# Row copies, load order and an early top-2 in a three-stage transformer kernel

## The chip, the cores and the metric

One core of one Trainium2 chip runs the whole program. The metric is the device time of one launch in microseconds (us). All tensors are float32 in DRAM.

## What is computed

Four sequences of 512 tokens of width 512 (2,048 rows) go through a mixture of experts, an attention layer, and the same mixture again, each with a residual sum:

```python
x = L0_attn_hidden_states                                     # (4, 512, 512)
x = x + 0.5 * ffn(layernorm(x), W_gate, b_gate, W_e, b_e)     # 8 experts, top 2
x = x + attn(layernorm(x), Wqkv, q_ln_w, q_ln_b, k_ln_w, k_ln_b, Wout)
x = x + 0.5 * ffn(layernorm(x), W_gate, b_gate, W_e, b_e)

# ffn: the two experts with the largest logits, their outputs averaged
logits = x @ W_gate + b_gate
_, top_idx = top_k(logits, 2)
y_all = relu(einsum('bsd,edh->bseh', x, W_e) + b_e)
y = take_along_axis(y_all, top_idx[..., None], axis=2).mean(axis=2)
# attn: 32 heads of 16, q and k clipped and layer-normed, ALiBi, causal softmax
```

## The kernel before

The program has three parts, each a block in which the five engines run their own instruction lists and meet at semaphores.

**First routing and first experts (0 to 238 us).** `route_block` (L1007, here with `proj` False) normalises the 16 tiles of 128 rows in 8 pairs and computes gate logits, the top 2, and lists that sort the (row, expert) pairs into 39 tiles of 128 slots. `expert_block` (L1588) gathers the normalised rows of a slot tile, multiplies them with one expert's weights and adds the result to the rows in `acc` with an indirect DMA. In the routing, SP's list (`sync`, L1188) does for pair u: load x for pair u+2 (L1128), store the normalised pair u-1 (L1145), load two pieces of expert weights (L1156), and store the raw pair u to `acc` (`store_x`, L1139), since the expert outputs are added there. A pair's buffer (4 of them, `XR`, which are the buffer of the expert biases) is loaded anew only when the store of its last content has landed (L1127). DVE's list (`vector`, L1453) does the statistics, 11 short steps of an inverse root, and two TENSOR_SCALARs (L1484) for each pair. ACT rounds each weight piece to its high part (L1404), and POOL subtracts it to get the low part (L1263), 16 pieces in all. PE transposes the pair (L1296), multiplies with the gate (`gate`, L1302) and turns the logits back (`turn_logits`, L1311), two pairs behind. When all 16 tiles have their logits, DVE picks the top 2 for all of them at once: 16 instructions (L1493 to L1507), and then PE ranks them (L1362 to L1365). The weights of the attention (`load_wq`, L1203) are loaded and turned in the gaps.

**Projection and attention (238 to 727 us).** `qkv_block` (L231) walks the 16 tiles. DVE's `unit(t)` (L478) begins with the statistics of the x tile t+2 (L485), which waits for that tile's load; then come the clip, the norms of q and k, and the normalised x of tile t+2. SP's `step(t)` (L310) does: store the four q and k pieces of tile t-2 (L308), load x of tile t+3 (L295), store v of tile t (L299). From tile 8 to 11 each step is followed by 14 DMAs that load a group's stacks (`load_fixed` with 6, L207, and `load` with 8, L218). `attention_block` (L571) walks NG = 32 groups of 4 heads. PE's iteration n (L806) has the scores with keys on partitions for group n (L758), the scores for the row maxima of group n+2 (L733), and the values of group n-1 (L771). The row maxima of group n+1 go: PE turns them (L742), ACT copies them to `m_rows` (L849), SP sends them into the q stack of that group by four small DMAs (`max_rows`, L631), and PE's first L758 of iteration n+1 waits for those (L749). SP's list for iteration n is: fixed rows of group n+4 (while n < 4), stack of group n+4, v of group n+2, `max_rows(n+1)`, and in some iterations a store (L639) and loads for the second routing (`sync_early`, L1163, from n = 16 to 24).

**Second routing and second experts (727 to 982 us).** The same functions with `proj` True: the routing also multiplies with the output weights and adds x (L1447), and stores the sum (L1141).

## Time and profile before

| | us |
|---|---|
| runs of the kernel before | 970.96, 975.37, 982.41 |
| median | 975.37 |
| profiled execution | 983.81 |
| its span from the first to the last record | 982.0 |
| PE busy in it | 841.5 |
| DVE, ACT, POOL busy in it | 632.4, 449.1, 446.1 |

The span begins with the first instruction that the profiler records and ends with the last one; 1.8 us of the execution lie around it. Busy time says little here, since the stages have different limits. Each stage is read by its own rows: which engine never waits, and who waits for whom at the step that is repeated.

### The profile page before, as it was taken

Reading aid. Unit: us, or ns where it says so; the run is one execution under the profiler, and the core shown is the slowest. Engines: PE = TensorE matmul, PEld = TensorE weight load, DVE = VectorE, ACT = ScalarE, POOL = GpSimd, SP = SyncE. Lnnn points to the kernel's source line nnn. Section 1 sums busy time; section 2 is a strip of 40 time slices with the busy share of each in tenths; the row PEclk is TensorE's granted clock in tenths of the full one; section 3 lists DMA queues with packets and bytes.
Section 4 is the critical chain, followed back from the end, with each engine's and each line's share of the span. In section 5 each row is a group of like instructions: output and inputs, shape, how many; then the busy total and the mean of one; then the engine's idle time right before and its main releaser. Section 6 shows DMA issues by size and latency. Waiting matters only on the chain. (4 is left out here: it accounts for less than half of the span.)

```text
span 982.0 us, 18936 instructions
## 1 busy us (share of the span) xinstructions
PE 841.5 (86%) x5922; PEld 592.5 (60%) x5923; DVE 632.4 (64%) x1289; ACT 449.1 (46%) x834; POOL 446.1 (45%) x565
## 2 busy tenths in 40 slices
PE   3666999993989998878899999889989983899995
PEld 1344888872677777655455555445557752788874
DVE  7966344333978877776688887678728768344432
ACT  3541333332244443347577777577754430233331
POOL 7732677764022222224243344235446431577764
PEclk9785999996899999978899999899999995899998
DMA  9985677863264689665667679898239940578874
GB/s 341 387 300 175 124 148 145 149 118 53 54 197 150 196 199 230 195 196 127 146 139 154 143 154 189 165 192 178 54 107 321 323 161 32 123 144 152 149 133 62
DMA packets 113255, 164.54 MB, mean 168 GB/s; under 512 B 16929, under 2 KB 74401, under 8 KB 112897
## 3 DMA queue, kind: packets, MB, share of 16 engines
q1 hardware_dynamic: 95328, 126.40, 46.6%
q0 software_dynamic: 17856, 37.25, 20.4%
q8 instruction: 39, 0.64, 0.3%
q14 instruction: 32, 0.25, 0.1%
HBM read 100.05 MB, written 68.68 MB: 172 GB/s over the span
## 5 line engine op out<-in xcount | busy, mean ns | idle before, releaser
L901 DVE TENSOR_REDUCE att_part<-att_s_ps 128x2 f32<-128x1024 f32 (+2 forms) x160 | 195.2, 1225 | 46.4 <-PE att_s_ps L733 42.4
L858 ACT ACTIVATE att_prob<-att_st_ps 128x512 f32<-128x512 f32 x320 | 174.2, 598 | 75.3 <-PE att_st_ps L758 71.2
L687 POOL TENSOR_SCALAR_AFFINE_SELECT att_prob<-att_prob 128x256 f32<-128x256 f32 (+1 forms) x224 | 93.7, 442 | 108.0 <-ACT att_prob L858 107.9
L153 PE MATMUL exp_z_ps<-ex_w_hi,exp_xT_hi 128*128 x312 | 132.4, 424 | 1.7 <-issue 1.3
L155 PE MATMUL exp_z_ps<-ex_w_hi,exp_xT_lo 128*128 x312 | 124.8, 400 | 0.0
L154 PE MATMUL exp_z_ps<-ex_w_lo,exp_xT_hi 128*128 x312 | 124.7, 400 | 0.0
L1684 ACT ACTIVATE exp_y<-exp_y 128x512 f32<-128x512 f32 x72 | 45.5, 632 | 170.5 <-DVE exp_y L1703 142.0
L1691 DVE TENSOR_TENSOR exp_xT_lo<-exp_t_ps,exp_xT_hi 128x512 fp32r<-128x512 f32 x78 | 53.9, 692 | 99.8 <-ACT exp_xT_hi L1675 81.2
L1263 POOL TENSOR_TENSOR ex_w_lo<-ex_w_lo,ex_w_hi 128x1024 fp32r<-128x1024 f32 x32 | 77.0, 2418 | 78.0 <-ACT ex_w_hi L1404 41.6
L771 PE MATMUL att_pv_ps<-att_prob,att_v_sb 128*32 128x256 f32 (+2 forms) x1280 | 103.2, 397 | 1.6 <-ACT wt_w_turned L863 1.6
L153 PE MATMUL qkv_o_ps<-qkv_w_hi,qkv_xT_hi 128*128 128x512 f32 x192 | 82.6, 430 | 2.4 <-DVE qkv_xT_lo L464 1.6
L154 PE MATMUL qkv_o_ps<-qkv_w_lo,qkv_xT_hi 128*128 128x512 f32 x192 | 78.6, 409 | 0.0
L155 PE MATMUL qkv_o_ps<-qkv_w_hi,qkv_xT_lo 128*128 128x512 f32 x192 | 78.0, 406 | 0.0
L1640 POOL DMA_INDIRECT out<-exp_y,ex_row_of x39 | 61.9, 1588 | 34.5 <-DMA out<-exp_y,ex_row_of 12.9
L363 POOL TENSOR_TENSOR st_partq<-qkv_wholeq,st_partq 128x512 fp32r<-128x512 f32 x16 | 20.7, 1293 | 124.9 <-ACT st_partq L435 124.9
L153 PEld LDWEIGHTS exp_z_ps<-ex_w_hi,exp_xT_hi 128*128 128x128 f32 x312 | 61.0, 195 | 15.7 <-issue 4.7
L155 PEld LDWEIGHTS exp_z_ps<-ex_w_hi,exp_xT_lo 128*128 128x128 f32 x312 | 60.0, 192 | 14.4
L1640 POOL DMA_INDIRECT acc<-exp_y,ex_row_of x33 | 52.4, 1589 | 33.4 <-issue 16.9
L154 PEld LDWEIGHTS exp_z_ps<-ex_w_lo,exp_xT_hi 128*128 128x128 f32 x312 | 60.5, 194 | 10.8
L712 PE MATMUL att_s_ps<-st_masks 64*128 64x256 bf16 (+1 forms) x640 | 58.9, 264 | 4.2 <-DVE att_part L901 4.2
L1675 ACT ACTIVATE exp_xT_hi<-exp_t_ps 128x512 fp32r<-128x512 f32 x78 | 45.4, 582 | 36.3 <-PE exp_t_ps L1652 36.3
L712 PEld LDWEIGHTS att_s_ps<-st_masks 64*128 64x128 bf16 x640 | 18.9, 97 | 61.5 <-issue 53.6
(206 smaller groups left out, 1618.2 us busy)
## 6 DMA issues: line engine op xcount, KB each, us to landing
ex_w_lo<-in_L_ffn_W_e SPq DMA_DIRECT2D x32, 512.0 KB, 6.7
v_vals<-st_vals SPq DMA_DIRECT2D x16, 512.0 KB, 2.9
q_parts<-st_partq SPq DMA_DIRECT2D x32, 256.0 KB, 3.6
k_parts<-st_partk SPq DMA_DIRECT2D x32, 256.0 KB, 4.0
att_v_sb<-v_vals SPq DMA_DIRECT2D x32, 256.0 KB, 3.8
ex_bias<-in_L_attn_hidden_states SPq DMA_DIRECT2D x8, 512.0 KB, 7.4
acc<-ex_bias SPq DMA_DIRECT2D x8, 512.0 KB, 8.3
xn<-ex_rows SPq DMA_DIRECT2D x8, 512.0 KB, 5.5
```

Of the source, the lines that this page charges most:

```text
L153: nc.tensor.matmul(out, x_hi[:, s], w_hi(c), start=(c == 0), stop=False)
L154: nc.tensor.matmul(out, x_hi[:, s], w_lo(c), start=False, stop=False)
L155: last = nc.tensor.matmul(out, x_lo[:, s], w_hi(c), start=False, stop=(c == C - 1))
L687: last = nc.gpsimd.affine_select(out=block, in_=block, compare_op=ALU.is_ge, fill=0.0, base=0, pattern=[[0, block.shape[1]], [1, P]], chan ...
L712: nc.tensor.matmul(blocks_of(banks[half], where), mine[:, 0, :], rhs, start=(c == 0), stop=False, skip_group_check=True)
L771: last = nc.tensor.matmul(pv_ps[VW * h:VW * (h + 1), j * P + c0:j * P + c1], v_sb[n % RING][:, j, VW * h:VW * (h + 1)], prob[n % 2][:, col ...
L858: nc.scalar.activation(prob[n % 2][:, col:col + 512], st_ps[(e + half) % 3][:, :], ACT.Exp).then_inc(exp_done, 1)
L901: nc.vector.tensor_reduce(out, src, X_AXIS, ALU.max, negate=True).then_inc(red_done, 1)
L1263: nc.gpsimd.tensor_tensor(ex.w_lo[:, 2 * n:2 * n + 2, :], ex.w_lo[:, 2 * n:2 * n + 2, :].bitcast(F32), ex.w_hi[:, 2 * n:2 * n + 2, :].bitc ...
L1640: nc.gpsimd.indirect_dma_start(out=acc[:, :], out_offset=bass.IndirectOffsetOnAxis(ap=ex.row_of[:, s:s + 1], axis=0), in_=y[s % RING], in_ ...
L1684: nc.scalar.activation(y[r], y[r], ACT.Relu, scale=0.25).then_inc(y_done, 1)
L1691: nc.vector.tensor_tensor(xT_lo[r % 2][:, :], t_ps[r % 2][:, :], xT_hi[r % 2][:, :].bitcast(F32), ALU.subtract).then_inc(lo_done, 1)
```

## The change

- **A.** First routing: `store_x` is gone from the loop. x rows reach `acc` by four DRAM-to-DRAM copies of 1 MB each (`copy_rows`), two behind the last store of normalised rows and two after the fourth piece of attention weights. The x loads no longer wait for stores, and neither does the load of the expert biases.
- **B.** Both routings: the top 2 are picked in two goes, for tiles 0 to 13 as soon as the seventh pair's logits are turned (after a copy of these logits to SBUF), and for tiles 14 and 15 after the last pair. PE turns the seventh pair's logits before it transposes the last pair. The buffer of the turned logits is now shared with the later one-hot columns and no longer with the picks.
- **C.** `qkv_block`: SP loads x of tile t+3 before it stores q and k of tile t-2.
- **D.** `attention_block`: `max_rows(n+1)` heads SP's iteration, before the stack and v loads, and takes two DMAs and not four; for this the maxima's high and low parts lie in another order in `m_parts`.

```diff
@@ qkv_block, sync @@
             def step(t, par):
+                if not (isinstance(t, int) and t + 3 >= TILES):
+                    load_x(t + 3, 1 - par)
                 if after(t, 2):
                     store_qk(t - 2, par)
-                if not (isinstance(t, int) and t + 3 >= TILES):
-                    load_x(t + 3, 1 - par)
                 store_v(t, par)
@@ attention_block, sync @@
                 for half, base in halves():
-                    for part_of in range(2):
-                        row = base + SCORE_ROWS + part_of
-                        src = m_rows[n % 2][4 * part_of + 2 * half:4 * part_of + 2 * half + 2, :]
-                        sp.dma_start(q_st[n % SLOTS][row:row + 1, :, :].bitcast(F32), src.bitcast(F32)).then_inc(m_loaded[n % 2], 16)
+                    row = base + SCORE_ROWS
+                    src = m_rows[n % 2][HG * half:HG * (half + 1), :]
+                    sp.dma_start(q_st[n % SLOTS][row:row + MAX_ROWS, :, :].bitcast(F32), src.bitcast(F32)).then_inc(m_loaded[n % 2], 16)
...
             for n in range(NG):
+                if n + 1 < NG:
+                    max_rows(n + 1)
                 if n + AHEAD < SLOTS:
                     st.load_fixed(sp, n + AHEAD)
                 if n + AHEAD < NG:
                     load(n + AHEAD)
                 if n + 2 < NG:
                     load_v(n + 2)
-                if n + 1 < NG:
-                    max_rows(n + 1)
@@ attention_block, gpsimd @@
-                flat = part[n % 2][:, :, :, :].rearrange("p a b s -> p (a b) s")
-                nc.gpsimd.tensor_copy(m_parts[n % 2][:, 0, :, :], flat).then_inc(m_hi_done, 1)
+                whole, parts = part[n % 2][:, :, :, :], m_parts[n % 2]
+                nc.gpsimd.tensor_copy(parts[:, :, 0, :, :], whole).then_inc(m_hi_done, 1)
                 pool.wait_ge(m_hi_done, n + 1)
-                nc.gpsimd.tensor_tensor(m_parts[n % 2][:, 1, :, :], flat, m_parts[n % 2][:, 0, :, :].bitcast(F32),
+                nc.gpsimd.tensor_tensor(parts[:, :, 1, :, :], whole, parts[:, :, 0, :, :].bitcast(F32),
                                         ALU.subtract).then_inc(m_lo_done, 1)
@@ route_block @@
-    lgT = work[0:E, 0:2 * P]
...
-    at_col = tables.sb("at_col", [P, COL_RING, P], BF16)
+    turning = tables.sb("turning", [P, 2 * P])
+    lgT = turning[0:E, :]
+    at_col = turning[:, :].bitcast(BF16).rearrange("p (r n) -> p r n", r=COL_RING)
...
     def load_x(u):
         if u >= XR:
             sp.wait_ge(xn_done, 2 * (u - XR) + 2)
-            sp.wait_ge(x_stored[u % XR], 16 * (u // XR))
+            if proj:
+                sp.wait_ge(x_stored[u % XR], 16 * (u // XR))
@@ route_block, sync @@
-            store_x(u)
+            if proj:
+                store_x(u)
...
+        def copy_rows(i):
+            part = slice(i * (TOKENS // XR), (i + 1) * (TOKENS // XR))
+            sp.dma_start(acc[part, :], x_in[part, :]).then_inc(x_stored[i], 16)
...
         store_xn(PAIRS - 1)
-        for i in range(XR):
-            sp.wait_ge(x_stored[i], 16 * (PAIRS // XR))
+        if not proj:
+            copy_rows(0)
+            copy_rows(1)
+        if proj:
+            for i in range(XR):
+                sp.wait_ge(x_stored[i], 16 * (PAIRS // XR))
         sp.wait_ge(xn_done, TILES)
         sp.dma_start(ex.bias[:, :], b_e.rearrange("(a e) h -> a (e h)", a=1).to_broadcast([P, E * D])).then_inc(ex.bias_loaded, 16)
         if w_qkv is not None:
-            for n in range(2, WQ_PAIRS):
-                load_wq(n)
+            load_wq(2)
+            load_wq(3)
+            copy_rows(2)
+            copy_rows(3)
+            load_wq(4)
+            load_wq(5)
@@ route_block, tensor @@
+            if u == PAIRS:
+                turn_logits(u - 2)
             if 1 <= u <= PAIRS:
                 transpose(2 * u - 2)
                 transpose(2 * u - 1)
-            if u >= 2:
+            if u >= 2 and u != PAIRS:
+                if u == PAIRS + 1:
+                    pe.wait_ge(lg_kept, 1)
                 turn_logits(u - 2)
@@ route_block, vector @@
+        kept = over[:, :, :].rearrange("p e t -> p (e t)").rearrange("p (t e) -> p t e", e=E)
+        def picks(t0, t1, first):
+            n, three = slice(t0, t1), [P, t1 - t0, E]
...
+            for k, source in enumerate((first, rest)):
+                chain(nc.vector.tensor_reduce(best[:, n, 0], source[:, n, :], X_AXIS, ALU.max))
+                chain(nc.vector.tensor_tensor(eq[:, n, :], source[:, n, :], best[:, n, :].to_broadcast(three), ALU.is_equal))
...
+            nc.vector.tensor_tensor(pair[:, n, 1, :], picked[:, n, :], pair[:, n, 0, :], ALU.subtract).then_inc(picked_done, 1)
+        dve.wait_ge(gate_done, PAIRS - 1)
+        nc.vector.tensor_copy(kept[:, 0:TILES - 2, :], logits[:, 0:TILES - 2, :]).then_inc(lg_kept, 1)
+        dve.wait_ge(lg_kept, 1)
+        picks(0, TILES - 2, kept)
         dve.wait_ge(gate_done, PAIRS)
...
+        picks(TILES - 2, TILES, logits)
```

`picks` has the 16 instructions of L1493 to L1507, each on tiles t0 to t1 only. The waits for `picked_done` (PE before the ranks, POOL before its last weight piece) now ask for 2 and not 1, and PE's and ACT's waits for `m_loaded` for 32 in each group and not 64.

## Rows read from the trace of the kernel before

**Rows 1.** Window 25 to 50 us: busy us of each engine, granted clock, DMA share, GB/s

```profile
25.00:50.00 25.00, 17.26 (x69) 8.52 (x68) 23.07 (x64) 13.25 (x20) 19.03 (x9) 0.73 0.99 380
```

**Rows 2.** Timeline of the routing loop: start us, us, engine, line, operation [idle before]

```profile
27.85 4.83 POOL L1263 TENSOR_TENSOR ex_w_lo<-ex_w_lo,ex_w_hi 128x1024 fp32r<-128x1024 f32 x2 [0.30 <-ACT ex_w_hi L1404]
...
29.32 3.65 DVE L1484 TENSOR_SCALAR ex_rows<-ex_bias,route_mv,route_rstd 128x512 f32<-128x512 f32 x2
...
57.21 1.00 DVE L1484 TENSOR_SCALAR ex_rows<-ex_bias,route_mv,route_rstd 128x512 f32<-128x512 f32 x2
```

**Rows 3.** 0 to 62 us: a group (busy, mean ns), a wait (total, times, longest)

```profile
L1484 DVE TENSOR_SCALAR ex_rows<-ex_bias,route_mv,route_rstd 128x512 f32<-128x512 f32 x16 | 21.8, 1403 | 0.3
...
ACT ex_w_hi L1404 <- DMA ex_w_lo<-in_L_ffn_W_e: 29.4, 9, 7.7
```

**Rows 4.** Timeline at the end of the first routing

```profile
59.95 0.29 PE L1315 MATMUL route_g_ps<-ex_ident,route_work 8*128 8x8 f32 x2
...
63.59 0.29 DVE L1493 TENSOR_REDUCE route_best<-route_g_ps 128x16 f32<-128x128 f32 x1 [5.38 <-PE route_g_ps L1315]
...
68.45 0.29 DVE L1507 TENSOR_TENSOR route_pair<-route_eq,route_pair 128x128 bf16<-128x128 f32 x1
...
71.34 0.17 DVE L1511 TENSOR_TENSOR route_counts<-route_totals 128x8 f32<-128x8 f32 x1
...
86.42 1.05 POOL L965 DMA_INDIRECT ex_rows<-xn,ex_token_of  x1 [15.19 <-DVE ex_token_of L1551]
```

**Rows 5.** Timeline at the end of the second routing: the first pick

```profile
810.60 0.29 DVE L1493 TENSOR_REDUCE route_best<-route_g_ps 128x16 f32<-128x128 f32 x1 [5.91 <-PE route_g_ps L1315]
```

**Rows 6.** DMA issues: a 2 MB copy within DRAM, us from issue to landing

```profile
bias_rows<-in_bias_rows SPq DMA_DIRECT2D x1, 8.8
```

**Rows 7.** Projection: SP's queue and DVE in time, tiles 7 to 9; last the total wait

```profile
339.30 0.34 SPq L299 DMA_DIRECT2D v_vals<-st_vals  x1
...
349.61 0.34 SPq L299 DMA_DIRECT2D v_vals<-st_vals  x1
...
356.07 0.98 SPq L308 DMA_DIRECT2D q_parts<-st_partq  x2
...
358.49 2.03 SPq L295 DMA_DIRECT2D qkv_x<-acc  x1
...
364.15 0.69 DVE L485 BATCH_NORM_STATS2 qkv_stats<-qkv_x 128x6 f32<-128x512 f32 x1 [4.18 <-DMA qkv_x<-acc]
...
DVE qkv_stats L485 <- DMA qkv_x<-acc: 14.0, 5, 4.2
```

**Rows 8.** Attention in time: ACT's maxima, SP's sending, PE's waits; last PE's total

```profile
457.38 0.57 ACT L849 ACTIVATE att_m_rows<-att_s_ps 8x512 fp32r<-8x512 f32 x1
...
474.91 0.57 ACT L849 ACTIVATE att_m_rows<-att_s_ps 8x512 fp32r<-8x512 f32 x1
...
478.69 2.38 SPq L637 DMA_DIRECT2D att_q_st<-att_m_rows  x4
...
482.22 0.79 PE L758 MATMUL att_st_ps<-att_q_st,att_k_st 64*128 64x512 f32 x2 [2.24 <-DMA att_q_st<-att_m_rows]
...
495.75 0.57 ACT L849 ACTIVATE att_m_rows<-att_s_ps 8x512 fp32r<-8x512 f32 x1
...
520.54 0.57 ACT L849 ACTIVATE att_m_rows<-att_s_ps 8x512 fp32r<-8x512 f32 x1
...
629.57 0.80 PE L758 MATMUL att_st_ps<-att_q_st,att_k_st 64*128 64x512 f32 x2 [3.28 <-DMA att_q_st<-att_m_rows]
...
711.00 0.57 ACT L849 ACTIVATE att_m_rows<-att_s_ps 8x512 fp32r<-8x512 f32 x1
...
  PE att_st_ps L758: 10.7, 9
```

**Rows 9.** Attention, windows without and with the routing's early weights (columns as Rows 1)

```profile
504.00:512.30 8.30, 7.87 (x103) 4.33 (x101) 6.87 (x8) 6.30 (x14) 3.33 (x10) 1.00 0.71 141
...
604.00:613.00 9.00, 8.01 (x108) 4.36 (x100) 6.98 (x9) 6.38 (x14) 3.40 (x9) 1.00 1.06 192
```

More of the change, by code:

```diff
@@ L581, in attention_block @@
         part = [m.sb(f"part{i}", [P, 2, 2, SEGS]) for i in range(2)]
-        m_parts = [m.sb(f"m_parts{i}", [P, 2, 4, SEGS], F32R) for i in range(2)]
+        m_parts = [m.sb(f"m_parts{i}", [P, 2, 2, 2, SEGS], F32R) for i in range(2)]
         m_rows = [m.sb(f"m_rows{i}", [2 * HG, SEQ], F32R) for i in range(2)]
@@ L607, in attention_block @@
         STACK_LOADS, FIXED_LOADS = 8, 6
+        MAX_LOADS = 16 * 2
         def ring_unit(k):
@@ L1489, in vector @@
         dve.wait_ge(const_done, 12)
-        dve.wait_ge(gate_done, PAIRS)
-        three = [P, TILES, E]
-        for k, source in enumerate((logits, rest)):
-            chain(nc.vector.tensor_reduce(best[:, :, 0], source[:, :, :], X_AXIS, ALU.max))
-            chain(nc.vector.tensor_tensor(eq[:, :, :], source[:, :, :], best[:, :, :].to_broadcast(three), ALU.is_equal))
-            chain(nc.vector.scalar_tensor_tensor(val[:, :, :], eq[:, :, :], -100.0, n_expert[:, :, :], ALU.mult, ALU.add))
-            chain(nc.vector.tensor_reduce(low[:, :, 0], val[:, :, :], X_AXIS, ALU.min))
-            chain(nc.vector.tensor_tensor(pick[k][:, :, :], val[:, :, :], low[:, :, :].to_broadcast(three), ALU.is_equal))
-            if k == 0:
-                chain(nc.vector.scalar_tensor_tensor(rest[:, :, :], pick[0][:, :, :], NEG, logits[:, :, :], ALU.mult, ALU.add))
@@ L1503, in vector @@
-        chain(nc.vector.tensor_tensor(picked[:, :, :], pick[0][:, :, :], pick[1][:, :, :], ALU.add))
-        chain(nc.vector.scalar_tensor_tensor(val[:, :, :], picked[:, :, :], -100.0, n_expert[:, :, :], ALU.mult, ALU.add))
-        chain(nc.vector.tensor_reduce(low[:, :, 0], val[:, :, :], X_AXIS, ALU.min))
-        chain(nc.vector.tensor_tensor(pair[:, :, 0, :], val[:, :, :], low[:, :, :].to_broadcast(three), ALU.is_equal))
-        nc.vector.tensor_tensor(pair[:, :, 1, :], picked[:, :, :], pair[:, :, 0, :], ALU.subtract).then_inc(picked_done, 1)
+        kept = over[:, :, :].rearrange("p e t -> p (e t)").rearrange("p (t e) -> p t e", e=E)
@@ new lines, in picks @@
+        def picks(t0, t1, first):
[3 more added lines that the diff above has]
+                chain(nc.vector.tensor_tensor(eq[:, n, :], source[:, n, :], best[:, n, :].to_broadcast(three), ALU.is_equal))
+                chain(nc.vector.scalar_tensor_tensor(val[:, n, :], eq[:, n, :], -100.0, n_expert[:, n, :], ALU.mult, ALU.add))
+                chain(nc.vector.tensor_reduce(low[:, n, 0], val[:, n, :], X_AXIS, ALU.min))
+                chain(nc.vector.tensor_tensor(pick[k][:, n, :], val[:, n, :], low[:, n, :].to_broadcast(three), ALU.is_equal))
+                if k == 0:
+                    chain(nc.vector.scalar_tensor_tensor(rest[:, n, :], pick[0][:, n, :], NEG, first[:, n, :], ALU.mult, ALU.add))
+            chain(nc.vector.tensor_tensor(picked[:, n, :], pick[0][:, n, :], pick[1][:, n, :], ALU.add))
+            chain(nc.vector.scalar_tensor_tensor(val[:, n, :], picked[:, n, :], -100.0, n_expert[:, n, :], ALU.mult, ALU.add))
+            chain(nc.vector.tensor_reduce(low[:, n, 0], val[:, n, :], X_AXIS, ALU.min))
+            chain(nc.vector.tensor_tensor(pair[:, n, 0, :], val[:, n, :], low[:, n, :].to_broadcast(three), ALU.is_equal))
+            nc.vector.tensor_tensor(pair[:, n, 1, :], picked[:, n, :], pair[:, n, 0, :], ALU.subtract).then_inc(picked_done, 1)
```

15 lines of the change are left out of this document (8 added, 7 removed).

## The prediction

> **What bounds the kernel now.** I read the windows first, then for each stage the waits, the timeline, and SP's queue.
>
> In the first routing DMA and DVE are both nearly full: 0.99 of the DMA engines' time and 23.07 of 25 us of DVE [rows 1]. The reader should see in the timeline which of them sets the end. DVE never waits in the loop after its first load; its normalising pair takes 1.00 us when POOL is idle, and 3.65 us when it starts inside two of POOL's weight pieces [rows 2]. All 16 TENSOR_SCALARs took 21.8 us [rows 3], at 0.50 us each it would be 8.0: 13.8 us of the loop is DVE standing behind POOL. DMA shows only as ACT's wait for weights, 29.4 us in nine [rows 3], off the path by itself. So the loop's end is set by DVE and POOL, not by the bytes.
>
> Behind the loop one chain runs to the first gather: logits, 16 picks from 63.59 to 68.74, ranks, lists, gather at 86.42 [rows 4]. The second routing has it too, from 810.60 on [rows 5].
>
> In the projection SP's v stores show the beat: 10.31 us for an undisturbed tile [rows 7]. Five times DVE waits for x, 14.0 us in all, 4.18 us at 364.15; that load was issued at 358.49, behind 14 stack loads and the q and k stores that began at 356.07 [rows 7].
>
> In the attention the undisturbed beat, from one of ACT's copies of maxima to the next, is 8.26 us (three from 495.75 to 520.54), with PE busy 7.87 of 8.30 us [rows 8, 9]. From 457.38 to 711.00 there are 29 beats in 253.6 us, 14.0 more than 29 x 8.26; the first four of them lose 5.3 (38.4 against 33.1) [rows 8]. PE waits nine times for maxima, 10.7 us, the longest 3.28 at 629.57 [rows 8]; this is most of the 14.0. There are two causes. At 478.69 SP sends maxima that ACT had ready at 475.48 [rows 8], since SP was still issuing 15 loads: late by 3.2 us. And in iterations with early weights the DMA share is 1.06 against 0.71 [rows 9], so the four small DMAs land behind a backlog.
>
> **A, the copies.** Removed: eight 512 KB stores. Added: four 1 MB copies. The 2 MB copy of the bias rows took 8.8 us from issue to landing [rows 6], so 4 MB are at most 17.6 us. They lie between 58 and 86 us beside 2 MB of biases and 2 MB of attention weights; these 8 MB at the loop's 380 GB/s [rows 1] are 22 us, which ends at about 80, before the gather at 86.42 [rows 4]. Cost nothing; if this cover is gone, the gather shares the engines with a tail of a few us, and I take 0 to +3. In the loop 4 of about 20 MB go, so weights land sooner and ACT and POOL start sooner; POOL still has its 15 pieces of 2.4 us. By the bytes the loop could shrink by 4.2 MB / 380 GB/s = 11 us; by the lock it shrinks only as far as fewer pieces fall on a pair. ACT's list puts the odd piece of each step behind the copies of the newest pair, so it still runs when the next pair is normalised, while the even piece can move ahead of it. So most of the 13.8 us stays: I take a fifth, rounded down to -2.5, with ends +2 (pieces can also fall worse, as the 3.65 shows) and -11.
>
> A rule that speaks against a gain by bytes stands in the Trainium skill, "SBUF — State Buffer", section "Who interferes with whom": VectorE and GpSimd share a pair of ports as an exclusive lock, and a TENSOR_SCALAR in its two-port mode blocks or is blocked for a whole instruction. By that rule the trace agrees (3.65 against 1.00 us), and A alone would give about nothing in the loop; by the bytes it would give 11.
>
> **B, the picks.** 16 instructions at 128x128 take 0.29 us, started every 0.32; at 16 columns they cost what L1511 does, 0.17 and 0.03 between, so 0.20 [rows 4]. The last go saves 16 x 0.12 = 1.9 us if the first go (a copy and 16 instructions at 112 columns, 5.2 us) fits before the last logits. Second routing: DVE is free at 804.69, since it idles 5.91 us before 810.60 [rows 5]; the first go ends at 809.9. It fits: -1.9. First routing: the seventh pair's logits were turned at 59.95 behind the transposes [rows 4], now at about 59.6; the first go ends at 65.1 and the second at 68.4, against 68.74. The transposes start 0.9 us later, but the last logits are still there in time. -0.3, up to -1.9 if the seventh gate product runs at 2.4 GHz: I take -0.7.
>
> **C, the x load.** SP would issue it at 356.07, not at 358.49, and 1 MB of stores is no longer ahead. Before, DVE had it 5.7 us after its issue [rows 7]; 1 MB at 380 GB/s is 2.8 us, so it takes about 3 and arrives near 359.0, where DVE wanted it at 359.97. What waits behind it on SP, the q and k stores, is wanted by nobody for two tiles; their engines have 10 us. So the 14.0 us should mostly go. But tiles 8 to 11 keep their 14 stack loads each, whose bytes are still ahead of x, and as the beats get shorter they press harder: I take 9 of the 14, ends -3 (only one of the five waits goes) and -12.
>
> **D, the maxima.** Two DMAs of the same kind save 2 x 0.6 = 1.2 us of SP's time per group (2.38 us for four [rows 8]). In iterations 0 to 3 SP issues 6 fixed, 8 stack and 1 v loads; the same 14 took 6.1 us in the projection (349.95 to 356.07 [rows 7]), 15 are 6.6, and with 2.4 that is 9.0 us against a beat of 8.26. With 7.8 us, and the maxima first, SP is never late: this gives back the 5.3 us. PE wants the maxima 4.5 us after ACT's copy (480.0 against 475.5 [rows 8]); in the iterations with early weights they have 3.3 us for landing then, not 2.1. The DMA share of 1.06 there [rows 9] says that a backlog stays, so of the other 8.7 us I take half, -4.3. POOL's two small instructions and PE's turn keep their sizes. D: -9.6, ends -3 and -14.
>
> The price of D: the stack of group n+4 and v are queued behind the wait for maxima n+1, some 6 us later than now. The stack is issued by 1.2 + 3.5 = 4.7 us after ACT's copy (7.3 with the fixed rows), and PE's L733 of group n+4 wants it a beat after the maxima, at 12.8. Cover: 8.1 us (5.5 in the first four) against 5.7 for a load behind a full queue [rows 7]. I cost it at nothing; without the cover each us late is a us in every group.
>
> **Sum.** -2.5 - 0.7 - 1.9 - 9 - 9.6 = -23.7 us on the profiled 983.8, that is 960.1, or 2.4%. The profiled execution is the slowest of the four times seen, and presumably has more of these waits; on the median of 975.4 I take nine tenths, 21 us: **954 us**.
>
> **Rivals.**
> 1. The backlog keeps the waits. For it: DMA share 1.06 [rows 9] and the full projection tiles; against it: the x load leaps over a megabyte. Only one x wait (14.0 / 5 = 2.8), SP's lateness (5.3) and B (2.6) are saved, about 11 us: 964.5 us.
> 2. Routing is DMA-bound after all and A gives its 11 us and not 2.5: 8.5 us more, 945.5 us. For it: 0.99; against it: DVE never idles.
> 3. Slower: the stacks come late (D). In iterations 0 to 27, each L733 of group n+2 would wait for its stack. It costs from a landing above 8.1 us after the last issue, and decides from 9.0, where 24 iterations eat the 21 us. At 9.6 it costs 36, and the kernel ends at 975.4 - 21 + 36 = 990 us. Against it: the 5.7 of [rows 7]; for it: the share of 1.06 [rows 9].
>
> The "Measured" table of the Trainium skill's "DMA: Bandwidth & Descriptors" (section "Bandwidth") gives 6.15 us for 1 MB, which puts the four copies at 24.6 us as an estimate, one after another; no run here shows it.
>
> **How the numbers follow.** My forecast 0.72, rival 1 0.17, rival 2 0.07, rival 3 0.04. The range 941 to 968 holds the first three with a few us around their times and leaves the slow case and the tails out, under 2 in 10. Some 1% (9.8 us) is what a measurement of this kernel can tell from no change. Faster by over 1% (below 965.6): the forecast, rival 2 and a third of rival 1, 0.85. Within 1%: 0.11. Slower: 0.04.
>
> **What would show it.** In the profile after: the picks of the last go at 0.17 us each, 3.3 us in all; DVE's wait at L485 below 4 us; SP's L637 in pairs of about 1.2 us right at ACT's copy; beats of 8.26 us in groups 2 to 6; L1484 at about 19 us in all. The prediction is wrong if L733 waits for stacks, if x waits stay near 14, or if the first gather starts before 78 or after 86.

## The result, and the profile after

The change makes the kernel about 1% faster, half of what was forecast. Each time is the median of whole launches; "before" is the kernel before on the same chip in the same stretch.

| | changed | before | ratio, 95% interval |
|---|---|---|---|
| first comparison | 970.23 us (10) | 982.23 us (10) | 0.9902 [0.9873, 0.9931] |
| run again beside the experiments (`again`) | 969.75 us (6) | 979.81 us (23) | 0.9882 [0.9843, 0.9920] |
| profiled execution of the first | 965.74 us, clock 0.936 | 983.81 us, clock 0.923 | |

The ratios leave out the executions that lie more than 1.5% above the fastest of their kernel, and so are not quite the quotients of these medians. By the ratios the change is worth 10 to 12 us. The pair of profiled executions differs by 18, since before's was a long one.

**First routing.** The group of the normalising pairs from 0 to 62 us (busy us, mean ns of one, idle before), and then the timeline of the changed kernel:

```profile
L1509 DVE TENSOR_SCALAR ex_rows<-ex_bias,route_mv,route_rstd 128x512 f32<-128x512 f32 x16 | 19.1, 1233 | 0.3
```

```profile
55.91 0.27 DVE L1520 TENSOR_REDUCE route_best<-route_over 128x14 f32<-128x112 f32 x1
...
59.80 0.26 PE L1335 MATMUL route_g_ps<-ex_ident,route_turning 8*128 8x8 f32 x2 [0.65 <-ACT route_turning L1425]
...
60.52 0.28 DVE L1533 TENSOR_TENSOR route_pair<-route_eq,route_pair 128x112 bf16<-128x112 f32 x1
60.71 0.17 DVE L1520 TENSOR_REDUCE route_best<-route_g_ps 128x2 f32<-128x16 f32 x1
...
63.82 0.17 DVE L1533 TENSOR_TENSOR route_pair<-route_eq,route_pair 128x16 bf16<-128x16 f32 x1
...
73.41 3.28 PE L1301 MATMUL route_wq_ps<-ex_ident,wo_turned 128*128 128x128 f32 x16 [8.04 <-DMA wo_turned<-in_L_attn_Wqkv]
```

L1509 is before's L1484: 21.8 us [rows 3] are now 19.1, the 2.5 of the forecast. It holds over all profiles: the 16 instructions take 22.6 us, added up, in the mean of the eight profiles without A (21.2 to 23.6) and 20.1 in the twelve with it (19.3 to 21.1). The last logits are there at 60.05 (L1335), and DVE is in its first go until 60.71, so the second go starts 0.7 us later than it could. The last picks take 0.17 us each and end at 64.0, where before's ended at 68.7 [rows 4]: 4.8 us earlier. But the first gather starts at 83.15 against 86.42, only 3.3 earlier. In between PE waits 8.04 us for a piece of the attention weights and comes late to the one-hot matmuls. From the end of the last pick to the first gather it is 17.4 to 17.7 us in the eight profiles without the copies, and 17.4 to 20.9, on average 19.5, in the eleven that have them as the change does: on average they take back 1.9 us.

**What follows the first gather.** POOL's first two gathers, SP's copy of the bias rows, and PE's transposes of the first two gathered tiles, changed kernel:

```profile
83.15 1.05 POOL L967 DMA_INDIRECT ex_rows<-xn,ex_token_of  x1 [16.67 <-DVE ex_token_of L1585]
83.71 0.51 SPq L1648 DMA_DIRECT2D bias_rows<-in_bias_rows  x1
84.50 0.97 POOL L967 DMA_INDIRECT ex_rows<-xn,ex_token_of  x1 [0.30 <-issue]
...
88.09 1.13 PE L1686 MATMUL exp_t_ps<-ex_ident,ex_rows 128*128 128x128 f32 x4 [4.57 <-DMA ex_rows<-xn,ex_token_of]
94.13 1.13 PE L1686 MATMUL exp_t_ps<-ex_ident,ex_rows 128*128 128x128 f32 x4 [4.91 <-DMA ex_rows<-xn,ex_token_of]
```

The same view of before, which the forecast had not looked at:

```profile
88.63 0.64 SPq L1614 DMA_DIRECT2D bias_rows<-in_bias_rows  x1
...
89.80 1.13 PE L1652 MATMUL exp_t_ps<-ex_ident,ex_rows 128*128 128x128 f32 x4 [1.36 <-DMA ex_rows<-xn,ex_token_of]
91.29 1.13 PE L1652 MATMUL exp_t_ps<-ex_ident,ex_rows 128*128 128x128 f32 x4 [0.37 <-DMA ex_rows<-xn,ex_token_of]
```

The second tile followed the first by 1.5 us; now by 6.0. By the start of the projection, 238.26 against 238.11, nothing of the earlier gather is left.

**Projection.** SP's x loads and v stores, the wait of DVE that follows, and then two totals of the waits from 345 to 410 us (us in total, times, longest):

```profile
353.18 0.42 SPq L295 DMA_DIRECT2D qkv_x<-acc  x1
...
364.63 0.42 SPq L295 DMA_DIRECT2D qkv_x<-acc  x1
365.10 0.98 SPq L308 DMA_DIRECT2D q_parts<-st_partq  x2
...
368.23 4.47 SPq L299 DMA_DIRECT2D v_vals<-st_vals  x1
...
372.75 0.69 DVE L485 BATCH_NORM_STATS2 qkv_stats<-qkv_x 128x6 f32<-128x512 f32 x1 [4.54 <-DMA qkv_x<-acc]
```

```profile
DVE qkv_stats L485 <- DMA qkv_x<-acc: 12.5, 4, 4.5
...
ACT st_partq L435 <- DMA k_parts<-st_partk: 6.5, 3, 3.4
```

SP does issue x ahead of the q and k stores now, and the issue itself takes 0.42 us where it took 2.03 [rows 7]. But the load lands 8.1 us after it (364.63 to 372.75), and the waits sum to 12.5 us in 4, against 14.0 in 5 [rows 7]. What was pushed back is the v store, whose issue takes 4.47 us. The one wait outside the tiles with stack loads, 2.4 us in the trace of before, is gone; the four within them were 11.6 us and are 12.5.

The DMA packets in the trace show what the load stands behind. The x of 364.63 is 128 packets of 2 KB. The first of them runs at 368.26, 3.6 us after the issue, and until then 104 packets of 4 KB, the size of those of the stack loads, have been started. These take 0.5 us each in the median from 363 to 370 us, where packets of 4 KB take 0.16 us from 360 to 362.

**Attention.** Two of ACT's copies of maxima, then PE's waits for them from 437 to 725 us (total, times, longest):

```profile
487.22 0.57 ACT L851 ACTIVATE att_m_rows<-att_s_ps 8x512 fp32r<-8x512 f32 x1
...
594.59 0.57 ACT L851 ACTIVATE att_m_rows<-att_s_ps 8x512 fp32r<-8x512 f32 x1
```

```profile
PE att_st_ps L760 <- DMA st_q<-att_m_rows: 1.7, 2, 1.5
```

Those are 13 beats in 107.4 us, 8.26 each. PE's 10.7 us in nine waits [rows 8] are 1.7 in two. This part went as the forecast says.

**Second routing.** The last pick of the last go:

```profile
798.16 0.17 DVE L1533 TENSOR_TENSOR route_pair<-route_eq,route_pair 128x16 bf16<-128x16 f32 x1
```

From the last copy of maxima (696.38) to it are 101.8 us, against 104.5 before (711.00 to 815.46). Over all profiles the means are 103.0 us in the twelve with B and 105.5 in the eight without.

### The profile page after: what moved, and what is told of

Same layout as the page of the kernel before. It is cut to its first block and busy times, and to the rows that moved or that the text cites. A ratio compares the mean times of both kernels' runs of the same rounds, so it can differ in the third digit from the quotient of the medians.

```text
span 964.0 us, 18898 instructions
## 1 busy us (share of the span) xinstructions
PE 828.3 (86%) x5922; PEld 586.6 (61%) x5923; DVE 635.7 (66%) x1323; ACT 447.8 (46%) x834; POOL 444.5 (46%) x565
## 5 line engine op out<-in xcount | busy, mean ns | idle before, releaser
L1725 DVE TENSOR_TENSOR exp_xT_lo<-exp_t_ps,exp_xT_hi 128x512 fp32r<-128x512 f32 x78 | 54.0, 692 | 103.0 <-ACT exp_xT_hi L1709 86.8
```

Of the source, the lines that this page charges most:

```text
L1725: nc.vector.tensor_tensor(xT_lo[r % 2][:, :], t_ps[r % 2][:, :], xT_hi[r % 2][:, :].bitcast(F32), ALU.subtract).then_inc(lo_done, 1)
```

## The experiments

One profile tells little of a microsecond here: over the 172 timed executions of the changed kernel and of all variants, each kernel's own mean taken off, 0.01 less of mean granted clock goes with 7.9 us more (correlation -0.71), and PE is busy for 828 us of the changed kernel. So times are ratios over 6 to 12 executions, and the profiles give places. Where the text says what a ratio is worth in us, it is multiplied by 980.

### The four parts alone, on the kernel before

Each takes its own hunks of the change and nothing else.

```diff
@@ only_a: the copies                       @@ only_b: the two goes of picks
-            sp.wait_ge(x_stored[u % XR], ...)   -   one go over 128x128
+        copy_rows(0) ... copy_rows(3)           +   picks(tiles 0-13); picks(tiles 14-15)
@@ only_c: load_x(t + 3) before store_qk    @@ only_d: max_rows first, two DMAs
```

> The kernel before with part A alone (copies within DRAM in the first routing). Theory 1, from the trace after: the loop ends 2 to 3 us earlier, but the attention weights land late behind the copies and the gain is gone before the projection starts; whole time within 2 us of before, first x load of the projection at 238 plus or minus 1. Theory 2, the prediction's: -2.5 us. Rival (the loop bound by bytes): -11 us.

> The kernel before with part B alone (top 2 in two goes, in both routings). Theory 1: the second routing gains 1.9 us (its last go at 0.17 us an instruction), the first at most 1; -2 to -3 us in all. Rival: more short instructions eat the gain, 0 us.

> The kernel before with part C alone (x load ahead of the q and k stores). Theory 1, from the trace after: the wait of DVE for x outside the tiles with stack loads goes, the four within them stay near 3 us each since the x load is still behind 14 stack loads; total wait 12 of 14.0 us, whole time -2 us. Theory 2, the prediction's: wait below 5 us, -9 us.

> The kernel before with part D alone (maxima first and in two DMAs). Theory 1, from the trace after: PE's waits for maxima fall from 10.7 us to about 2, beats of 8.26 us nearly throughout, -9 to -12 us: D carries most of the whole change. Theory 2: as predicted, half of the backlog's waits stay, -9.6 us in a profile like before's and less in a median run. Rival (late stacks): slower.

| | median (n) | ratio, 95% interval | worth |
|---|---|---|---|
| only_a | 979.54 (12) | 1.0005 [0.9971, 1.0040] | +0.5 us |
| only_b | 978.42 (12) | 1.0004 [0.9963, 1.0045] | +0.4 |
| only_c | 977.85 (12) | 1.0005 [0.9971, 1.0039] | +0.5 |
| only_d | 973.42 (12) | 0.9934 [0.9896, 0.9971] | -6.5 |

Only D shows alone. In only_c the L485 waits were 13.9 us in four, and the x loads landed up to 8.9 us after their issue. So C is the term that is missing most. Terms of 2.5 us, as A's and B's, cannot be told from nothing in intervals 7 to 8 us wide.

### The gain of A and B, and the copy of the bias rows

SP issues the copy of the bias rows (2 MB within DRAM, L1614 before, L1648 after) when PE has turned the last attention weights, whatever POOL does. `bias_late` puts it behind the first four gathers in the changed kernel, `before_bl` in the kernel before, `ab_bl` in before with A and B. `ab` is before with A and B alone, and `again` the changed kernel unaltered.

```diff
                 copied = m.sem("copied")
+                for s in range(C):
+                    sp.wait_ge(gathered[s], 16)
```

> The changed kernel with the 2 MB copy of the bias rows issued only when the first four gathers have landed. In the changed kernel the copy was issued 0.56 us after the first gather, and the second gather's rows reached PE 6.0 us after the first's (88.09 and 94.13), against 1.5 us in the profile of before (89.80 and 91.29), where the copy came 2.2 us after the first gather and stood behind two of them. If that copy delays the gathers: second expert transpose within 2 us of the first, first add at 98 us instead of 102.88, and the time lower by 3 to 5 us. Rival: the gathers are bound by something else, or the copy delays the expert weights or the later gathers instead: the add stays at 102 to 103 or the gain is lost by 238 us (the start of the projection), and the time is the same within 1 us.

> The kernel before with one edit: the copy of the bias rows waits until the first four gathers have landed. In the five profiles with the first routing of before, or near to it, in which the copy was issued within 1.5 us of the first gather, the second gather's rows came 7 to 9 us behind the first's; in the profile of before and in that of only_c, where it came 2.2 us after, 1.5 us behind. If the kernel before falls on the bad side in most of its executions: ratio 0.993 to 0.996 (4 to 6 us), second expert transpose within 2 us of the first. If before is mostly on the good side as its profile was: ratio 0.999 to 1.001.

> The kernel before with A and B and with the copy of the bias rows behind the first four gathers; to be read against before_bl, which differs by A and B alone. Theory: A and B save their 3 to 5 us (loop 2.5 us, picks 0.7 and 1.9) and in the change it was given back since the copy of the bias rows then fell right behind the first gather: ab_bl is 3 to 5 us under before_bl, with the first add 3 us earlier. Rival: A's copies cost in the routing what the loop gains (PE waited 8.0 us for the attention weights' third piece in the changed kernel): ab_bl is within 2 us of before_bl.

> A and B together on the kernel before, without the edit on the bias rows; ab_bl had 970.7 us (0.9930). Theory, the routing's gain is given back to the copy of the bias rows in the first 230 us and the second routing keeps its 2 us: ratio 0.997 to 0.999, 3 to 5 us above ab_bl, second expert transpose 5 to 9 us behind the first. Rival, A and B keep their gain without help: 0.993 to 0.995, as ab_bl.

> The changed kernel once more, unaltered, in one group with ab, c_early and d_two. First measured 970.2 us at a ratio of 0.9902 [0.9873, 0.9931]. Theory: its time is 965 to 972 us, and in its profile the second expert transpose follows the first by 5 to 9 us whenever the copy of the bias rows is issued less than 1.5 us behind the first gather, and by 1.5 us otherwise. Rival: the spacing does not follow the issue time, and the reading of the copy falls.

| | median (n) | ratio, 95% interval |
|---|---|---|
| bias_late | 958.95 (6) | 0.9783 [0.9744, 0.9822] |
| before_bl | 976.65 (12) | 0.9963 [0.9929, 0.9997] |
| ab_bl | 970.66 (12) | 0.9930 [0.9891, 0.9969] |
| ab | 976.19 (12) | 0.9965 [0.9931, 0.9998] |
| again | 969.75 (6) | 0.9882 [0.9843, 0.9920] |

The timeline of `again`, as above: the copy is issued 1.29 us behind the first gather, and the second transpose comes 9.05 us behind the first.

```profile
84.63 1.05 POOL L967 DMA_INDIRECT ex_rows<-xn,ex_token_of  x1 [16.99 <-DVE ex_token_of L1585]
85.92 0.51 SPq L1648 DMA_DIRECT2D bias_rows<-in_bias_rows  x1
...
97.07 1.13 PE L1686 MATMUL exp_t_ps<-ex_ident,ex_rows 128*128 128x128 f32 x4 [7.92 <-DMA ex_rows<-xn,ex_token_of]
```

And `bias_late`, where the copy goes out at 91.60:

```profile
84.02 1.05 POOL L967 DMA_INDIRECT ex_rows<-xn,ex_token_of  x1 [14.93 <-DVE ex_token_of L1585]
...
87.48 0.87 PE L1688 MATMUL exp_t_ps<-ex_ident,ex_rows 128*128 128x128 f32 x4 [2.11 <-DMA ex_rows<-xn,ex_token_of]
88.95 1.13 PE L1688 MATMUL exp_t_ps<-ex_ident,ex_rows 128*128 128x128 f32 x4 [0.60 <-DMA ex_rows<-xn,ex_token_of]
```

The profiles of all kernels, in three groups by when the copy was issued behind the start of the first gather:

| copy issued after the first gather | profiles | second transpose behind the first | first gather to the start of the projection |
|---|---|---|---|
| 0.56 to 1.79 us | 8: after, again, only_a, only_b, only_d, d_order, x_early, c_early | 5.8 to 9.1 us | mean 155.2 us (153.3 to 157.9) |
| 1.96 to 2.22 us | 5: before, only_c, ab, d_two, spread | 1.5 to 2.2 us | mean 150.8 (149.6 to 151.7) |
| behind four gathers | 7: bias_late, before_bl, ab_bl, all3, all4, x_bl, spread_bl | 1.4 to 1.6 us | mean 148.8 (147.1 to 150.4) |

No profile breaks the order of the first group and the other two; the last column of the second and the third overlaps. By the means, whether the second gather gets out ahead of the copy decides 4.4 us, and keeping the copy back altogether 6.4. My expectation for `again` put the edge at 1.5 us; c_early, at 1.79, was still on the bad side. Of the six profiles whose first routing is before's, three fell on it (only_d, d_order, c_early) and three did not (before, only_c, d_two), so it is no mark of the changed kernel.

What sets the distance in these profiles is TensorE's clock. PE's last piece of the attention weights, 16 transposes, begins 1.6 us before the first gather in all thirteen profiles of the first two groups, and the copy is issued when that piece is done. The piece in the changed kernel and in before (columns as in [rows 1]):

```profile
81.58:83.52 1.94, 1.94 (x17) 1.70 (x16) 1.64 (x6) 1.28 (x3) 0.37 (x1) 1.00 0.00 1
```

```profile
84.79:88.44 3.65, 3.65 (x18) 3.25 (x17) 3.08 (x12) 1.79 (x3) 1.72 (x2) 0.50 0.10 20
```

At a granted clock of 1.00 (2.4 GHz) it takes 1.94 us and the copy goes out 0.56 us behind the gather; so in x_early. At 0.50 (1.2 GHz) it takes 3.65 us and the copy goes out 2.21 us behind; so in only_c and spread. In the other eight the clock changes within the piece, it takes 2.7 to 3.5 us, and the copy follows 1.29 to 2.07 us behind, in the same order. Before the piece PE had been busy for 3.8 us (81.00 to 84.79) in before and for 8.0 of 8.2 (73.41 to 81.58) in the changed kernel.

For before_bl I had expected 0.993 to 0.996 if before is mostly on the bad side, 0.999 to 1.001 if on the good. The measured 0.9963 lies between, next to the first, and its interval reaches into both. ab_bl against before_bl is A and B with the copy out of the way: 6.0 us by the medians, 3.2 by the ratios. ab against before, with the copy in play, is 3.4 us by its ratio; I had expected 1 to 3 us and the second transpose 5 to 9 us behind the first, and in its profile that was 2.2. So the gain of A and B is 3 to 6 us against the 5.1 forecast, and what the copy takes from it is not told apart by the times; the profiles put it at 4.4 us whenever it strikes.

bias_late beat its expectation: 11 us under the changed kernel by the medians, where 3 to 5 were expected. The first add is at 97.72 (98 was expected, 102.88 is the changed kernel's). In the profiles the start of the projection is 5.5 us earlier than in the first profile of the changed kernel and 6.8 earlier than in `again`. Of the rest I can only say that the median execution had a clock of 0.939 against 0.934 to 0.935. Why is open.

### The x load in the projection

`x_early` is the changed kernel with the load a tile earlier, ahead of the v store and the stack loads; `c_early` the kernel before with the load at that same place. `spread` leaves C as it is and spreads the 14 stack loads of a tile over two.

```diff
@@ x_early, c_early @@                          @@ spread @@
-  load_x(t + 3, 1 - par)                      -  if t < TILES // 2 + AHEAD:
   store_qk(t - 2, par)                        -      st.load_fixed(sp, n); st.load(sp, n)
+  load_x(t + 4, par)                          +  n, part = divmod(t - TILES // 2, 2)
   store_v(t, par)                             +  load_fixed(n) if part == 0 else load(n)
```

> The changed kernel with the x loads issued one tile earlier still: ahead of the v store and of the stack loads of the same tile, so that no stack load stands between the free buffer and the load. Theory 1, the wait is the late issue plus the 5.4 to 8.1 us of landing: the L485 waits (12.5 us in the changed kernel) fall under 2 us, tiles 8 to 11 come back to about 10.5 us each, and the time falls by 8 to 12 us. Theory 2, those four tiles are bound by what the DMA engines carry (DMA share 1.10, 1.06 and 0.98 in three of them): the L485 waits go too, but the time shows again in ACT's wait for the k store and in PE's or DVE's waits behind it; the four tiles together keep at least half of their 12.5 us, and the time falls by 0 to 5 us.

> The changed kernel with the 14 stack loads of a group spread over two tiles: 6 fixed loads in tiles 8, 10, 12, 14 and 8 stack loads in tiles 9, 11, 13, 15, in place of 14 in each of tiles 8 to 11. The order of x is the changed kernel's. If the backlog of 14 loads in front of x makes the wait: L485 waits under 4 us in all, SP's v store issues under 1 us each, the stage shorter by 8 to 12 us, and PE's first score products at most 2 us later behind the last tile. Rival: bytes have only moved, tiles 9, 11, 13 and 15 wait 2 to 3 us each, and the time falls by 0 to 3 us; or the last group's stack is late for the attention, which would show as PE waiting for a stack there and give it all back.

> The kernel before with C alone, and the x load a tile earlier than C has it. C alone gave 1.0005. Theory, the waits for x are worth their size when the load leaves before the stack loads: L485 waits under 2 us in all, from the start of the projection to the first copy of maxima 186 to 189 us where only_c had 200.0, and the ratio is 0.988 to 0.992, 8 to 11 us under only_c. Rival, on the kernel before the next beat is held by something else (SP behind its four maxima DMAs, the attention's first stacks): ratio 0.995 to 1.000.

| | median (n) | ratio, 95% interval | L485 waits | start of projection to first maxima |
|---|---|---|---|---|
| x_early | 952.77 (6) | 0.9718 [0.9674, 0.9762] | 0 | 186.2 us |
| spread | 958.96 (6) | 0.9781 [0.9739, 0.9822] | 0 | 187.3 |
| c_early | 967.73 (6) | 0.9868 [0.9822, 0.9913] | 0 | 187.2 |
| only_c (above) | 977.85 (12) | 1.0005 [0.9971, 1.0039] | 13.9, in 4 | 200.0 |
| changed | | | 12.5, in 4 | 196.8 |

In x_early SP's queue reads as follows, at the place of 364.63 above; behind it ACT's wait for the k stores, over the stage:

```profile
367.09 2.42 SPq L295 DMA_DIRECT2D qkv_x<-acc  x1
369.56 0.43 SPq L299 DMA_DIRECT2D v_vals<-st_vals  x1
```

```profile
ACT st_partq L436 <- DMA k_parts<-st_partk: 10.2, 3, 5.3
```

This x is wanted only at 378, by the tile after next. It still stands behind the stack loads of the tile before and lands 6.0 us after its issue; in three tiles x lands after 5.6 to 6.7. The load has not become faster, it has a tile more time. The backlog has not gone either: ACT waits 10.2 us for k stores. It has moved to engines that have the time. The two stretches of four tiles between the same two L485 instructions, changed kernel and then x_early (columns as in [rows 1]):

```profile
346.60:398.10 51.50, 42.07 (x196) 33.04 (x195) 34.40 (x98) 19.27 (x44) 10.33 (x8) 0.97 1.00 213
```

```profile
346.90:388.40 41.50, 39.74 (x194) 31.71 (x193) 36.90 (x97) 19.17 (x44) 10.57 (x8) 1.00 0.97 234
```

A DMA share of 1.00 at 213 GB/s looked like a bound, and theory 2 rested on it. The same work went through in 10 us less at 0.97 and 234 GB/s. In spread the last eight x loads land 2.8 to 3.8 us after their issue, median 3.3 (changed: 2.9 to 8.1). That is nearly the forecast's "about 3", and it comes with 6 or 8 stack loads ahead, not with 14. c_early against only_c is 13 us by the ratios: the waits, 13.9 us, were worth their size, but C was not the edit that removes them.

From the start of the projection to the first maxima x_early is 10.6 us shorter than the changed kernel; 8 to 12 were expected for the whole. The medians differ by 17. The rest is not explained; the median of the granted clock is 0.94 against 0.934.

### Which half of D

> The kernel before with one edit: SP issues the maxima of the next group ahead of the early loads, still as four DMAs; POOL and PE keep their old forms. D as a whole gave 0.9934 timed, and its attention took 259.0 us from the first copy of maxima to the last against 273.9, 271.4, 264.6 and 268.5 in the four profiles without it. If the order carries D: beats of 8.26 us, 259 to 261 us for the 31 beats, a ratio of 0.992 to 0.996, and PE's waits for maxima under 2 us in all. Rival: the two DMAs saved per group carry it, since 2.4 us of issues still stand ahead of the early loads: then PE's waits stay at 7 to 10 us, the 31 beats at 264 to 270 us, and the ratio is 1.000.

> The kernel before with the other half of D: two DMAs for the maxima of a group in place of four, POOL writing them in the order that this needs, and SP issuing them in the old place, behind the early loads. D gave 0.9934, the new place alone 0.9985 [0.9948, 1.0021]. If the two halves add: 0.995. If D needs both (two DMAs fit the beat of the first four groups only together with the new place): 0.998 to 1.000, with PE waiting for maxima 6 us or more in all. If the fewer DMAs carry it: 0.993 to 0.995, waits under 2 us.

```diff
@@ d_order: place alone @@              @@ d_two: number alone @@
+  max_rows(n + 1)   # before load()    -  for part_of in range(2): ... 4 dma_start
-  max_rows(n + 1)   # after load_v()   +  2 dma_start of MAX_ROWS rows
```

| | median (n) | ratio, 95% interval | 31 beats | PE's waits for maxima |
|---|---|---|---|---|
| d_order | 978.98 (12) | 0.9985 [0.9948, 1.0021] | 269.1 us | 7.8 us in 6 |
| d_two | 974.01 (12) | 0.9915 [0.9877, 0.9953] | 262.2 | 1.9 in 1 |
| only_d | 973.42 (12) | 0.9934 [0.9896, 0.9971] | 259.0 | 0.7 in 2 |

The number carries it. The place alone shows nothing that can be measured: its interval allows 5 us, but its 31 beats are those of the eight profiles with four DMAs in the old place, 264.6 to 273.9 us. In d_order (its profiled execution is the longest of the twelve), ACT has the maxima at 490.37; SP, which sends them first in its iteration, comes to it 4.4 us later, still busy with the iteration before; PE waits:

```profile
490.37 0.57 ACT L850 ACTIVATE att_m_rows<-att_s_ps 8x512 fp32r<-8x512 f32 x1
...
494.79 2.40 SPq L637 DMA_DIRECT2D att_q_st<-att_m_rows  x4
...
498.33 0.80 PE L759 MATMUL att_st_ps<-att_q_st,att_k_st 64*128 64x512 f32 x2 [2.90 <-DMA att_q_st<-att_m_rows]
```

In d_two, with the old place, SP is there in time:

```profile
477.27 0.57 ACT L850 ACTIVATE att_m_rows<-att_s_ps 8x512 fp32r<-8x512 f32 x1
...
477.87 1.30 SPq L637 DMA_DIRECT2D att_q_st<-att_m_rows  x2
```

In the first groups a queue with 9.0 us of work in a beat of 8.26 is late wherever an item stands in it; at 7.8 it is in time in either place. 5.0 of d_order's 7.8 us of waits lie there. In the groups with early weights it waits 2.8 us, against 2.9 to 8.0 in the eight profiles just named, so there the place may help; one profile does not tell.

### All together

> The changed kernel with all three edits that were run alone on it: x loads a tile earlier (952.8 us), stack loads spread over two tiles (959.0) and bias rows behind the gathers (959.0), beside 970.2 of the changed kernel. The first two remove the same waits of 12.5 us, the third another wait. If the waits are separate as read: 17.5 + 5 to 11 below 970, that is 942 to 948 us. Rival: the spread loads only move the backlog (PE then misses its stacks in the first groups), and the result is 950 to 953, as x_early alone.

> As all3, and in the first routing ACT issues the third and fourth piece of the attention weights behind the first 1 MB copy alone, and the other three copies after them. PE's wait for that piece (8.0 us in the changed kernel, 4.6 to 8.9 in the variants) falls under 3 us. If that wait is on the path of the one-hot matmuls: 1 to 2 us less than all3. Rival: the last copy of rows now lands behind the weights and the first gather waits for it, 0 to 3 us more than all3.

> The changed kernel with the x loads a tile earlier and the bias rows behind the gathers, the stack loads not spread. If the spreading takes something back in all3 (its profile had waits for maxima of 2 us in the attention, that of x_early none): 943 to 948 us. If the two savings overlap or part of either was in the clock that the chip granted (0.934 in the median execution of the changed kernel, 0.939 in both variants, and 0.01 of clock goes with 8 us): 949 to 953 us.

> The changed kernel with the stack loads spread over two tiles and the bias rows behind the gathers, x as in the change. spread alone: 959.0 us in the median, but 947.9 in its profiled execution, the one where the copy of the bias rows was issued 2.2 us behind the first gather and the second transpose followed the first by 1.7 us. If most executions of spread fall on the bad side: 950 to 954 us. If the spacing is worth nothing: 957 to 960 us.

```diff
@@ all4, beside all3's three edits @@
-        copy_rows(0); copy_rows(1)     # behind the last store
+            copy_rows(0)
             load_wq(2); load_wq(3)
+            copy_rows(1)
             copy_rows(2); copy_rows(3)
```

| | edits on the changed kernel | median (n) | ratio, 95% interval |
|---|---|---|---|
| x_early | x earlier | 952.77 (6) | 0.9718 [0.9674, 0.9762] |
| x_bl | x earlier, bias rows late | 954.00 (6) | 0.9761 [0.9712, 0.9811] |
| spread_bl | spread, bias rows late | 954.53 (6) | 0.9764 [0.9713, 0.9816] |
| all3 | all three | 951.85 (6) | 0.9727 [0.9673, 0.9781] |
| all4 | all three, weights before copies | 951.76 (6) | 0.9709 [0.9656, 0.9763] |

The savings do not add: 17 and 11 us alone, 16 together in x_bl and 18 in all3. x_bl against x_early excludes that the spreading takes it back. In x_bl's profile the second transpose follows the first by 1.4 us and the projection starts 3.8 us earlier than in x_early's, so the saving is there in place, but the whole is no shorter: from the first maxima on, x_bl takes 529.6 us and x_early 525.8. 1.6 us of that lie between the last copy of maxima and the last pick of the second routing; what causes it I cannot name. spread_bl, expected at 950 to 954, is 4 us under spread by its median and 2 by its ratio, too little to say on which side most executions of spread fell. In all4, PE's waits for the attention weights are 3.1 us (8.0 in all3) and the first gather starts at 81.67 (83.79), much as expected; the time does not show it. All these variants are 2.4 to 2.9% under before and 15 to 18 us under the changed kernel.

## Why the prediction was wrong

The sign and the mechanism of D were right; the size was twice too large, and the median lies 16 us above 954 and 2 above the range. 4 to 7 of the 16 us come from the starting point: the forecast stood on a median of 975.4 us from three runs, and before's medians beside the changed kernel are 979.8 and 982.2. The other 9 to 12 are the change's own.

- **C, -9 us: the step that failed.** "... so it takes about 3 and arrives near 359.0": it arrived 5.3 to 8.1 us after its issue. I had counted the megabyte of stores that no longer stood ahead, and named the 14 stack loads as a mere pressure for which 5 of the 14 us were left. They are nearly all of it: in their four tiles the waits went from 11.6 us to 12.5. C alone measured +0.5 us [-2.8, +3.8]. The forecast had the warning in its own rows: 5.7 us after its issue for 256 KB, with 14 loads ahead of it in both orders. The Trainium skill says in "DMA: Bandwidth & Descriptors", section "Queues, rings and completion order", that the DMAs of one issuing engine share one ring on each DMA engine and are consumed in ring order; the trace agrees: the x of 364.63 has its first packet 3.6 us after its issue, behind those of the stack loads, and x lands after 5.3 to 8.1 us behind 14 of them against 2.8 to 3.8 in spread.
- **D, -9.6 us: right, somewhat large.** -6.5 us [-10.2, -2.8] timed. Over all profiles the 31 beats take 268.9 us on average in the nine without the two DMAs (264.6 to 273.9) and 260.4 in the ten with all of D: 8.5. The profiled before, 273.9, was the worst of the nine, so a sum made on it was too high; nine tenths did not correct enough. The reason given for the first four groups, 9.0 us of SP's issues against 8.26, is what d_two and d_order show; that the maxima must also go first is not borne out. No L733 waited for a stack.
- **A, -2.5 us in the loop: right in place.** 21.8 to 19.1 us. The lock argument held: by the bytes it would have been 11. The Trainium skill's rule ("SBUF — State Buffer", "Who interferes with whom") would have A alone give about nothing, and 2.7 is nearer to that. **"Cost nothing" for the copies: wrong.** The bytes were counted well: the last copy landed at 79.6 us, the forecast had about 80. But the copies took up to 16.6 us to land, PE waited 8.04 us for weights behind them, and 1.5 of the 4.8 us gained at the last pick were lost by the first gather; the mean over all profiles, 1.9 us, is most of what A gains in the loop. The cover I had named, up to the gather at 86.42, was that of the copies' own readers; the weights queued behind them have an earlier reader.
- **B, -2.6 us: right as a sum, by some luck.** 16 picks at 0.17 us. The first go did not fit: it ended 0.7 to 0.8 us after the last logits in both routings of the changed kernel's profile. From the last logits to the end of the last pick it was 5.3 us in both routings before, and is 3.9 and 4.1 now, a gain of 1.3 and 1.2 where 0.7 and 1.9 were forecast. Together A and B measured -3.4 us [-6.8, -0.2].
- **What no step had: the copy of the bias rows.** It goes out when PE has turned the last weights, the gather 1.6 us after PE begins to. The granted clock in that piece sets how far apart they are, 0.56 to 2.2 us, and which comes first is worth 4.4 us. It struck three of five profiles of kernels with A and B, and three of six of kernels with neither, so it is scatter of both and no shown cost of the change.
- **The sum.** Measured alone: -3.4 (A and B) + 0.5 (C) - 6.5 (D) = -9.4 us; measured together -10 to -12. The parts add, within what they can be measured to, and the failed term is C's 9 of the missing 10 or so; D is short by 3 and A and B by 2, within their intervals.
- **The rivals.** Rival 1 gave 11 us and came nearest, on half its grounds: the backlog kept the x waits, but not those for maxima. Rivals 2 and 3 did not come. The signals named for "wrong" included x waits near 14, and that is the one that came true; the first gather at 83.15, the picks at 0.17 us, the beats of 8.26 and L1484's 19 us all came as named.

## What to carry to other kernels

When a load is moved forward in an issue queue, count what still stands ahead of it there, and take its landing time from a row with the same things ahead; moving it past four stores was worth nothing here, since fourteen loads remained. Before shortening a stage, list the large transfers whose start hangs on another engine's progress, and make them wait for the small latency-bound ones that they can overtake. Sums of waits read from one profiled execution have to be set against several executions: here one stage of 31 beats varied by 9 us between profiles of equal code.

## What the runs showed of the hardware

- A 2 MB copy within DRAM that is issued up to 1.79 us behind the first of several indirect gathers holds the second one's rows back by 4 to 7.5 us; issued 1.96 us or more behind it, so that the second gather is out as well, it holds them back by 0.8 us at most, and the third gather's instead: PE's third transpose comes 7.3 us behind the second in before and 6.2 in bias_late. The Trainium skill ("DMA: Bandwidth & Descriptors", "Queues, rings and completion order") has each DMA engine take turns between its queues packet by packet. The trace agrees, and the packets explain the size. The changed kernel from 84 to 91 us (packets, MB, share of the 16 engines' time):

```profile
q1 hardware_dynamic: 32, 2.10, 72.1%
q0 software_dynamic: 87, 0.29, 22.1%
```

  The copy (q1) is 32 packets of 64 KB, which take 2.5 us each; the gathers (q0) go in packets of 4 KB, which take 0.16 us in the median. A gather of 256 KB has 64 of them, four for each of 16 engines if they are spread evenly, and the copy two. By turns, these two stand before the gather's last packet: an estimate of 5 us, against the 4 to 7.5 measured.
- The same 16 transposes of 128x128 float32 took PE 3.65 us at a granted clock of 0.50 and 1.94 us at 1.00.
- A stretch with a DMA share of 1.00 was not bound by DMA: the same four tiles ran in 41.5 us and not 51.5 when one load stood elsewhere in the queue. The share counts the time that packets take, and in the changed kernel one of 4 KB took 0.16 us from 360 to 362 us and 0.5 from 363 to 370.
- SP's issue of a v store takes 0.34 us in most tiles, and up to 4.47 us in the changed kernel and 5.35 in only_c behind 14 stack loads, the x load and four stores. In before's order, where x comes last of these, it is the issue of x that takes 2.0 to 2.3 us. So a backlog shows in the issue times of whatever comes next on that engine.
